# A recommender tower on one core: sums of a tile taken in PSUM, products on Pool, layer 0 spread out, six Y banks

## The chip, the cores and the metric

The kernel runs on one core of a Trainium2 chip. The metric is the device time of one execution in microseconds. Before the change it is 732.16 us, the median of three runs (731.63 to 733.88).

## The reference, cut to what matters

For each of 512 samples, 40 embedding rows of 16 numbers are gathered from 40 tables (`e`, 512 x 40 x 16). Three layers follow, then a small dense network:

```
x = e
for k in (k0, k1, k2):                      # k0: 128x40x40, k1 and k2: 128x128x40
    x = einsum('bhd,bmd,ohm->bod', x, e, k) # outer product with e, mixed by k
    outputs.append(x.sum(-1))
h = concat(outputs + [dense_ctx])           # 512 x (3*128 + 16)
h = relu(h @ W_top1 + b1); h = relu(h @ W_top2 + b2); y = h @ W_top3
```

All data is fp32.

## The kernel before, in words

A token is a pair (sample, d); there are 8192. They are worked in 16 groups of 512 tokens (32 samples), a group in four tiles of 128 tokens, so 64 tiles T.

Per group, the preparation: Pool gathers the rows (ten indirect DMAs per group, L220); SP stores them into a scratch in HBM (six DMAs, L188), and loads them back (L191, L196) as A3 (the 40 fields three times, 120 rows) and as seven rolled copies `pairs`. DVE multiplies each copy with A3 (L359), which gives all products of two fields. Layer 0 is seven matmuls into the bank X1: three of them split into a high and a low fp32r part (L280 on ACT, L366 on DVE, three passes each at L475 to L477), four in plain fp32 (L481, two passes each). X1 is then split into x1hi (ACT, L283) and x1lo (DVE, L370), and summed over d into z0 (DVE, L373). PE also transposes A3 into xtok (L462, L271), the token's 40 field values as per-partition scalars.

Per tile, layer 1: ten chunks c0 to c9 of 512 columns (four m by 128 outputs). Each is three fp32r matmuls into one of five PSUM banks Y (L515 to L517). Each quarter of a chunk is then multiplied by its xtok scalar and all 40 quarters are summed. ACT owns six chunks (OWNER "ADAADAADAD") and writes the scaled values to SBUF (`scaled`, L318). DVE owns four and accumulates as it multiplies (L427). Pool adds three of ACT's results (`fold`, L257), and DVE merges all into x2 (L392, four steps). Then G = x2 against a diagonal pattern `diag` (Pool, L247) gives, per sample, what layer 2 and the sums need: two half-height matmuls (L491), copied by ACT (L286).

The steps of the next group's preparation are dealt into the stream of chunks by a table of positions (`position`, `prep_steps`): p counts a group's 40 chunks on each engine. A hardware loop runs three bodies of four groups; the fourth body stands unrolled behind it. After the last group, layer 2 and the dense network follow (L531 to L557).

What orders the engines are counting semaphores: chunk c of a tile may not start before its bank's earlier chunk has been read; s_l0, s_x1free and s_xtok guard X1, TR and xtok; s_merge, s_diag and s_Gout guard G.

Of the kernel before, what the change touches and what calls it, by code (L numbers as in the profile page):

```python
# [30 lines left out]
NA, ND = OWNER.count("A"), OWNER.count("D")
STT = ND * MB
FOLDS = 3
EXTRA = NA - 2 - FOLDS
MERGE = EXTRA + 3
NS = 3
# [2 lines left out]
XTOK_AT, PROD_AT, PROD_APART, L0_LAG = 14, 6, 3.6, 6
SPLIT_LAG = {"ph": 1, "pl": 2}  # L40
X1_LAG = {"x1hi": 1, "x1lo": 2, "z0": 3}
GATHER_TILES = 3
MERGE_AT = (0, 3, 3, 3)
G_AT = 8
def position(step):
    if step == "xtok":
        return XTOK_AT
    if step in X1_LAG:
        return position(f"l0_{NC0 - 1}") + X1_LAG[step]
    kind, c = step[:-1], int(step[-1])  # L50
    if kind in ("l0_", "prod"):
        return int(PROD_AT + PROD_APART * c) + (L0_LAG if kind == "l0_" else 0)
    return int(PROD_AT + PROD_APART * c) + SPLIT_LAG[kind]
def prep_steps():
    names = ["xtok"]
    for kind, n in (("prod", NC0), ("ph", NS), ("pl", NS), ("l0_", NC0)):
        names += [f"{kind}{c}" for c in range(n)]
    names += X1_LAG
    return sorted(names, key=position)
def rank(c):  # L60
    return OWNER[:c + 1].count(OWNER[c])
def chunk(u, slot, c):
    k = NC0 * (slot + 1) + c
    return GPB * NC0 * u + k, k % NR, GPB * NC0 // NR * u + k // NR
def split(u, slot, c):
    k = NS * (slot + 1) + c
    number = NC0 * (GPB * u + slot + 1) + c
    free = number - NH + 1 if c >= NH else number - NC0 + NS - NH + 1 if slot >= 0 else None
    return GPB * NS * u + k, k % NH, free
def build(nc, ids, first_row, table, k0a, k0b, k1, k2, ctxT, w1, w1c, b1, w2, b2, w3, ident_in, mask_in,  # L70
# [7 lines left out]
    with ctx:  # L78
# [24 lines left out]
        scaled = sb("scaled", [P, NA, BANK])  # L103
        fold = [sb(f"fold{i}", [P, BANK]) for i in range(2)]
        chain = [sb(f"chain{i}", [P, BANK]) for i in range(2)]
# [1 line left out]
        diag = [sb(f"diag{i}", [P, MH, HB]) for i in range(2)]
        G = sb("G", [P, MH, SB + B])
# [496 lines left out]
```

## Time and profile before

| | us |
|---|---|
| median of the runs | 732.16 |
| the profiled execution | 735.69 |
| its span | 733.9 |
| PE busy | 672.8 (92%) |
| DVE busy | 609.3 (83%) |
| POOL busy | 526.9 (72%) |
| ACT busy | 520.1 (71%) |

One execution was profiled. Busy times of an engine are unions, so overlapping instructions count once. PE busy includes the modelled ends of pipelined matmuls. A stretch of the loop is best read from the first Y matmul of one group (L515) to that of the next.

### The profile page before, as it was taken

How to read it: one execution, taken by the hardware profiler on the slowest of the kernel's cores; microseconds unless marked ns; L12 is line 12 of the kernel's file. 1: busy time of each engine (PE TensorE's matmuls, PEld its weight loads, DVE VectorE, ACT ScalarE, POOL GpSimd, SP SyncE). 2: the span in 40 equal slices, each digit the busy share in tenths (PEclk: the TensorE clock that was granted, in tenths of full speed). 3: DMA queues.
4: the chain of work that ended last, by engine and by line, in shares of the span. 5: the costliest groups of instructions: out<-in, count | busy, mean ns of one | idle time of the engine just before them, and what ended most of it. 6: DMA issues, size and time to landing. Idle time of an engine off the chain costs nothing.

```text
span 733.9 us, 13319 instructions
## 1 busy us (share of the span) xinstructions
PE 672.8 (92%) x2752; PEld 472.9 (64%) x2752; DVE 609.3 (83%) x1542; ACT 520.1 (71%) x1753; POOL 526.9 (72%) x443
## 2 busy tenths in 40 slices
PE   0379999999989999999999999999999999998998
PEld 0246767677666766676667767676767676773583
DVE  1649898888989898989798998989898989888290
ACT  1338777777777777778777777687778787886293
POOL 6538888998979798988789888888797874552000
PEclk9999999999999999999999999999999999997799
DMA  6361120302031212122120303031312121100000
GB/s 203 98 232 50 37 83 13 108 10 97 20 89 29 79 40 76 44 59 60 26 95 10 96 19 100 17 90 29 84 36 78 43 77 41 47 1 29 0 1 0
DMA packets 56679, 43.08 MB, mean 59 GB/s; under 512 B 37007, under 2 KB 40335, under 8 KB 56352
## 3 DMA queue, kind: packets, MB, share of 16 engines
q1 hardware_dynamic: 51488, 41.08, 18.5%
q0 software_dynamic: 5120, 1.32, 1.9%
q14 instruction: 59, 0.48, 0.2%
q8 instruction: 12, 0.20, 0.1%
HBM read 40.41 MB, written 1.97 MB: 58 GB/s over the span
## 4 chain that ended last, share of the span: by engine, by line
issue 33%; POOL 29%; PE 27%; DVE 6%; DMA 3%; SPq 1%; POOLq 1%; ACT 1%; DVEq 0%; ACTq 0%
POOL x0g L220 17%; POOL fold L257 9%; PE Y L515 5%; PE Y L517 5%; PE Y L516 5%; DVE chain L427 2%; POOL diag L247 2%; PE X L481 2%; DMA pairs<-scratch 2%; DVE pairs L359 1%; PE X L542 1%; PE X L540 1%; PE X L541 1%; DVE chain L392 1%; PE GB L491 1%
## 5 line engine op out<-in xcount | busy, mean ns | idle before, releaser
L318 ACT ACTIVATE scaled<-Y,xtok 128x128 f32<-128x128 f32 x1536 | 421.1, 380 | 107.1 <-PE Y L517 106.3
L515 PE MATMUL Y<-k1lo,x1hi 128*128 128x512 f32 x640 | 290.4, 454 | 20.1 <-DVE chain L427 18.6
L517 PE MATMUL Y<-k1hi,x1lo 128*128 128x512 f32 x640 | 253.1, 396 | 0.0
L516 PE MATMUL Y<-k1hi,x1hi 128*128 128x512 f32 x640 | 252.5, 395 | 0.0
L220 POOL DMA_INDIRECT x0g<-in_table,rows_now x160 | 221.0, 1381 | 42.2 <-issue 37.8
L427 DVE SCALAR_TENSOR_TENSOR chain<-Y,xtok,chain 128x128 f32<-128x128 f32 x768 | 213.0, 339 | 23.7 <-PE Y L517 23.7
L257 POOL TENSOR_TENSOR fold<-fold,scaled 128x512 f32<-128x512 f32 x128 | 183.8, 1436 | 12.5 <-ACT scaled L318 0.6
L515 PEld LDWEIGHTS Y<-k1lo,x1hi 128*128 128x128 f32 x640 | 120.5, 188 | 80.4 <-DVE chain L427 37.0
L516 PEld LDWEIGHTS Y<-k1hi,x1hi 128*128 128x128 f32 x640 | 121.0, 189 | 35.6 <-issue 14.4
L517 PEld LDWEIGHTS Y<-k1hi,x1lo 128*128 128x128 f32 x640 | 120.6, 188 | 30.3
L359 DVE TENSOR_TENSOR pairs<-pairs,A 120x512 f32<-120x512 f32 x112 | 108.9, 973 | 30.9 <-DMA pairs<-scratch 30.9
L257 POOL TENSOR_TENSOR fold<-scaled 128x512 f32<-128x512 f32 x64 | 84.4, 1318 | 68.7 <-ACT scaled L318 68.7
L427 DVE SCALAR_TENSOR_TENSOR chain<-Y,xtok,scaled 128x128 f32<-128x128 f32 x256 | 71.8, 342 | 5.1 <-PE Y L517 4.0
L481 PE MATMUL X<-pairs,w 120*128 120x512 f32 x128 | 65.6, 594 | 1.7 <-DVE pairs L359 1.7
L280 ACT ACTIVATE pairs_hi<-pairs 120x512 fp32r<-120x512 f32 x48 | 30.3, 632 | 47.5 <-DVE pairs L359 47.5
L392 DVE TENSOR_TENSOR chain<-chain,scaled 128x512 f32<-128x512 f32 x65 | 44.9, 691 | 7.9 <-ACT scaled L318 4.8
L475 PE MATMUL X<-pairs_lo,w0hi 120*128 120x512 f32 x48 | 22.6, 470 | 30.2 <-DVE pairs_lo L366 30.2
L392 DVE TENSOR_TENSOR chain<-chain,fold 128x512 f32<-128x512 f32 x65 | 44.3, 681 | 0.0
L366 DVE TENSOR_TENSOR pairs_lo<-pairs,pairs_hi 120x512 fp32r<-120x512 f32 x48 | 40.5, 843 | 3.0 <-ACT pairs_hi L280 3.0
L491 PE MATMUL GB<-diag,x 64*128 64x164 f32 x260 | 36.1, 354 | 6.2 <-DVE x L392 6.2
L491 PEld LDWEIGHTS GB<-diag,x 64*128 64x128 f32 x260 | 19.8, 186 | 30.3 <-issue 22.3
L247 POOL TENSOR_TENSOR diag<-xtok,mask 128x160 f32<-128x160 f32 x64 | 35.5, 555 | 2.8 <-POOL rows_now L216 1.9
(77 smaller groups left out, 460.3 us busy)
## 6 DMA issues: line engine op xcount, KB each, us to landing
pairs<-scratch SPq DMA_DIRECT2D x112, 240.0 KB
A<-scratch SPq DMA_DIRECT2D x16, 240.0 KB
k1raw<-in_k SPq DMA_DIRECT2D x1, 2560.0 KB, 10.8
x0g<-in_table,rows_now POOLq DMA_INDIRECT x160, 2.8
k2s<-in_k SPq DMA_DIRECT2D x1, 2560.0 KB, 9.2
scratch<-x0g SPq DMA_DIRECT2D x96, 20.0 KB, 1.7
pairs<-in_w SPq DMA_DIRECT2D x3, 256.0 KB, 3.0
w2s<-in_w SPq DMA_DIRECT2D x1, 512.0 KB, 3.9
```

The costliest lines, as they stand in the source:

```text
L220: nc.gpsimd.indirect_dma_start(x0g[buf][:, f, :], None, table, bass.IndirectOffsetOnAxis(ap=rows_now[buf][:, f:f + 1], axis=0)).then_inc(s ...
L247: nc.gpsimd.tensor_tensor(diag[tile % 2][:, 0:M, :], xtok[slot % 2][:, j, :].unsqueeze(2).to_broadcast([P, M, HB]), mask[:, :].unsqueeze(1 ...
L257: nc.gpsimd.tensor_tensor(sums[:, :], scaled[:, 1, :] if a == 2 else sums[:, :], scaled[:, a, :], ALU.add).then_inc(s_fold, 1)
L318: ins = nc.scalar.activation(scaled[:, rank(c) - 1, i * O:(i + 1) * O], Y[(NCH * tile + c) % YB][:, i * O:(i + 1) * O], ACT.Copy, scale=xt ...
L359: nc.vector.tensor_tensor(pairs[buf][0:PR, :], pairs[buf][0:PR, :], A3[par][0:PR, :], ALU.mult).then_inc(s_prod, 1)
L392: nc.vector.tensor_tensor(to, a, b, ALU.add).then_inc(s_merge, 1)
L427: nc.vector.scalar_tensor_tensor(out=chain[tile % 2][:, i * O:(i + 1) * O], in0=Y[(NCH * tile + c) % YB][:, i * O:(i + 1) * O], scalar=xto ...
L481: nc.tensor.matmul(X1[:, :], w0[:, (c - NS) * O:(c - NS + 1) * O], pairs[buf][0:PR, :], start=False, stop=(c == NC0 - 1)).then_inc(s_l0, 1)
L491: ins = nc.tensor.matmul(GB2[:, h, 0:MH * HB], x2[buf][rows, :], diag[buf][rows, :, :].rearrange("p m b -> p (m b)"), start=True, stop=True)
L515: nc.tensor.matmul(y, hi[:, tok], k1lo[:, cols], start=True, stop=False)
L516: nc.tensor.matmul(y, hi[:, tok], k1hi[:, cols], start=False, stop=False)
L517: nc.tensor.matmul(y, lo[:, tok], k1hi[:, cols], start=False, stop=True).then_inc(s_y, 1)
```

## The change

The loop is gone: all 64 tiles are written out. There are six Y banks; G has one bank, and the transposes go through X1 (`TR = X1`). ACT owns seven chunks (OWNER "AADAAADAAD": 0, 1, 3, 4, 5, 7, 8), DVE three (2, 6, 9). ACT scales chunk 0 into SBUF (`first`) and the other six in place, in their PSUM banks. DVE starts with chunk 2 on top of `first`, adds ACT's chunks straight from PSUM, and ends with chunk 9, whose four quarters it writes back into the bank and reduces into x2. Pool no longer folds; it makes the products of the next group (of the first group, DVE does) and a `diag` of double width for one full-height G matmul. Layer 0 is seven plain fp32 matmuls at chunks 5, 9, 14, 18, 22, 27, 31 of the group before. `pairs` has seven buffers. At the start, ACT issues half of the first group's stores and loads, and PE runs 20 matmuls on k1hi whose results are not used. k2s is loaded after group 2's loads.

```diff
-YB = 5
-OWNER = "ADAADAADAD"
+YB = 6
+OWNER = "AADAAADAAD"
+WARM = 20
+XTOK_PE_AT, XTOK_AT = 1, 3
+L0_AT = (5, 9, 14, 18, 22, 27, 31)
+X1HI_AT = 33
+G_AT, GCOPY_AT = 4, 5
+PRODUCTS_OF_TILE = ((0, 1, 2), (3, 4, 5), (6,), ())
+GATHERS_OF_TILE = ((0, 3), (3, 6), (6, 10), (0, 0))
+STEPS = ("mac2", "mac2", "mac2", "mac2", "sum1", "sum3", "sum4", "mac6", "mac6", "mac6", "mac6", "sum5",
+         "sum7", "sum8", "mac9", "mac9", "mac9", "mac9", "quarters")
...
 @block.sync
+            for r in range(0, ROLLS // GF, 2):
+                store_copy(sp, 0, r)
+            sp.wait_ge(s_scratch, 16 * (ROLLS // GF))
+            sp.dma_start(A3[0][0:PR, :], rolled_rows(0, 0, 0)).then_inc(s_a3, 16)
+            for c in range(0, NC0, 2):
+                load_roll(sp, 0, c)
...
 @block.gpsimd
+            for g in range(NG):
+                for j in range(TPG):
+                    T = TPG * g + j
+                    pool.wait_ge(s_xtok, g + 1)
+                    if T >= 2:
+                        pool.wait_ge(s_G, T - 1)
+                    nc.gpsimd.tensor_tensor(diag[T % 2][:, 0:M, :], ...
+                    if j == 0 and g + 2 < NG:
+                        take_rows(g + 2, g % 2)
+                    if g + 1 < NG:
+                        for c in PRODUCTS_OF_TILE[j]:
+                            product(g + 1, c)
+                    if g + 2 < NG:
+                        gather(g % 2, range(*GATHERS_OF_TILE[j]))
...
 @block.scalar
+                        for i in range(MB):
+                            m, o = c * MB + i, slice(i * O, (i + 1) * O)
+                            ins = nc.scalar.activation(first[:, o] if c == 0 else y[:, o], y[:, o], ACT.Copy,
+                                                       scale=xtok[g % 2][:, j, m:m + 1])
...
 @block.vector
+            def add_scaled(T, c):
+                dve.wait_ge(s_yA, act_count(T, c))
+                nc.vector.tensor_tensor(chain[:, :], chain[:, :], Y[(NCH * T + c) % YB][:, :],
+                                        ALU.add).then_inc(s_chain, 1)
...
+                nc.vector.tensor_reduce(x2[T % 2][:, :], Y[(NCH * T + 9) % YB][:, :].rearrange(
+                    "p (m o) -> p o m", o=O), AX.X, ALU.add).then_inc(s_chain, 1)
...
 @block.tensor
+                    if k >= YB:
+                        wait_for_bank(k)
...
+                        if p == XTOK_PE_AT:
+                            pe.wait_ge(s_a3, 16 * (g + 2))
+                            pe.wait_ge(s_x1free, g + 1)
+                            transposes(g + 1)
+                        elif p in L0_AT:
+                            if p == L0_AT[0]:
+                                pe.wait_ge(s_xtok, g + 2)
+                            pe.wait_ge(s_prod, NC0 * g + L0_AT.index(p) + 1)
+                            layer0(L0_AT.index(p))
+                    if c == G_AT and T > 0:
+                        make_G(T - 1)
```

How the instructions stand on DVE at the end of a group, first before (the group's last tile up to the next group's first multiply-adds; chain1 and chain0 are the sums of the two tiles, Y the banks, fold1 Pool's sum):

```order
L427 SCALAR_TENSOR_TENSOR chain1<-Y4,xtok1,chain1 128x128 [waits chain_steps,y_filled]
L427 SCALAR_TENSOR_TENSOR chain1<-Y4,xtok1,chain1 128x128 [waits chain_steps] x3
L370 TENSOR_TENSOR x1lo0<-X1,x1hi0 128x512 [waits x1_high_ready]
L373 TENSOR_REDUCE z0<-X1 128x32
L427 SCALAR_TENSOR_TENSOR chain1<-Y2,xtok1,chain1 128x128 [waits chain_steps,y_filled]
L427 SCALAR_TENSOR_TENSOR chain1<-Y2,xtok1,chain1 128x128 [waits chain_steps] x3
L427 SCALAR_TENSOR_TENSOR chain1<-Y4,xtok1,chain1 128x128 [waits chain_steps,y_filled]
L427 SCALAR_TENSOR_TENSOR chain1<-Y4,xtok1,chain1 128x128 [waits chain_steps] x3
L392 TENSOR_TENSOR chain1<-chain1,scaled 128x512 [waits y_emptied_by_act,chain_steps]
```

Now the same place, from chunk 6 of the group's last tile on (chain is the one sum, Y3 at the end the bank of chunk 9):

```order
L338 TENSOR_TENSOR chain<-chain,Y4 128x512 [waits y_scaled_by_act,chain_steps]
L332 SCALAR_TENSOR_TENSOR chain<-Y0,xtok1,chain 128x128 [waits y_filled,chain_steps]
L332 SCALAR_TENSOR_TENSOR chain<-Y0,xtok1,chain 128x128 x3
L302 TENSOR_TENSOR x1lo0<-X1,x1hi0 128x512 [waits x1_high_ready]
L338 TENSOR_TENSOR chain<-chain,Y5 128x512 [waits y_scaled_by_act,chain_steps]
L338 TENSOR_TENSOR chain<-chain,Y1 128x512 [waits y_scaled_by_act,chain_steps]
L305 TENSOR_REDUCE z0<-X1 128x32
L338 TENSOR_TENSOR chain<-chain,Y2 128x512 [waits y_scaled_by_act,chain_steps]
L332 SCALAR_TENSOR_TENSOR Y3<-Y3,xtok1,chain 128x128 [waits y_filled,chain_steps]
L332 SCALAR_TENSOR_TENSOR Y3<-Y3,xtok1,chain 128x128 x3
L370 TENSOR_REDUCE x2_1<-Y3 128x128 [waits g_filled,chain_steps]
```

Before, only the tile's own multiply-adds on chunk 4 stand ahead of x1lo, with z0 right behind it. Now the adds of ACT's chunks 1, 3 and 4 (the last of them is the first row) and the multiply-adds on chunk 6 stand ahead of x1lo, and two more adds ahead of z0.

On ACT, x1hi in the group's last tile, before:

```order
L318 ACTIVATE scaled<-Y2,xtok1 128x128 [waits y_filled,pool_folds]
L318 ACTIVATE scaled<-Y2,xtok1 128x128 x3
L318 ACTIVATE scaled<-Y3,xtok1 128x128 [waits y_filled,pool_folds]
L318 ACTIVATE scaled<-Y3,xtok1 128x128 x3
L283 ACTIVATE x1hi0<-X1 128x512 [waits l0_done]
L318 ACTIVATE scaled<-Y0,xtok1 128x128 [waits y_filled,pool_folds]
L318 ACTIVATE scaled<-Y0,xtok1 128x128 x3
```

and now:

```order
L265 ACTIVATE first<-Y0,xtok0 128x128 [waits y_filled,chain_steps]
L265 ACTIVATE first<-Y0,xtok0 128x128 x3
L265 ACTIVATE Y1<-Y1,xtok0 128x128 [waits y_filled]
L265 ACTIVATE Y1<-Y1,xtok0 128x128 x3
L265 ACTIVATE Y3<-Y3,xtok0 128x128 [waits y_filled]
L265 ACTIVATE Y3<-Y3,xtok0 128x128 x3
L229 ACTIVATE x1hi1<-X1 128x512 [waits l0_done]
L265 ACTIVATE Y4<-Y4,xtok0 128x128 [waits y_filled]
L265 ACTIVATE Y4<-Y4,xtok0 128x128 x3
```

x1hi is behind chunk 3 both times; the chunks beside it now go back to their own banks and wait for no fold.

## Rows read from the trace of the kernel before

**Rows 1.** Busy times by stretch: five groups, the work behind the last G

```profile
43.67:84.47 40.80, 39.35 (x161) 28.41 (x162) 33.82 (x89) 29.50 (x105) 31.51 (x24) 0.96 0.26 73
162.89:202.09 39.20, 37.88 (x163) 27.24 (x161) 35.28 (x92) 29.80 (x106) 33.77 (x27) 1.00 0.20 57
202.09:242.89 40.80, 37.90 (x162) 27.32 (x161) 36.45 (x92) 29.86 (x106) 33.88 (x27) 1.00 0.20 55
556.97:595.09 38.12, 37.75 (x162) 27.16 (x161) 35.03 (x92) 29.79 (x107) 31.11 (x28) 1.00 0.21 59
634.02:668.36 34.34, 30.89 (x137) 23.23 (x135) 28.89 (x89) 30.25 (x107) 17.89 (x17) 0.99 0.07 24
668.36:733.90 65.54, 62.63 (x176) 33.85 (x176) 33.43 (x50) 33.24 (x54) 0.00 (x0) 0.85 0.03 8
```

Columns: stretch, its length, busy us (and instructions) of PE, PEld, DVE, ACT, POOL, granted clock, share of the DMA engines, GB/s.

**Rows 2.** The same view, the first and the fourth tile of one group

```profile
162.89:170.57 7.68, 7.68 (x36) 5.86 (x34) 5.27 (x17) 5.71 (x21) 5.35 (x6) 1.00 0.41 118
192.69:202.09 9.40, 9.40 (x40) 6.62 (x38) 8.04 (x23) 7.38 (x27) 8.44 (x7) 1.00 0.07 9
```

**Rows 3.** Timeline, PE, one chunk and the next one's start (start, us, instruction)

```profile
162.89 0.40 PE L515 MATMUL Y<-k1lo,x1hi 128*128 128x512 f32 x1
...
163.36 0.39 PE L517 MATMUL Y<-k1hi,x1lo 128*128 128x512 f32 x1
163.59 0.40 PE L515 MATMUL Y<-k1lo,x1hi 128*128 128x512 f32 x1
```

**Rows 4.** Timeline, the end of the last tile and the last G

```profile
664.94 1.13 DVE L427 SCALAR_TENSOR_TENSOR chain<-Y,xtok,chain 128x128 f32<-128x128 f32 x4 [0.96 <-PE Y L517]
...
666.11 0.69 DVE L392 TENSOR_TENSOR chain<-chain,scaled 128x512 f32<-128x512 f32 x1
666.83 0.69 DVE L392 TENSOR_TENSOR chain<-chain,fold 128x512 f32<-128x512 f32 x1
...
668.36 0.92 PE L491 MATMUL GB<-diag,x 64*128 64x164 f32 x4 [3.46 <-DVE x L392]
```

**Rows 5.** Groups of instructions by line and shape (busy us, mean ns | idle before)

```profile
L318 ACT ACTIVATE scaled<-Y,xtok 128x128 f32<-128x128 f32 x1536 | 421.1, 380 | 107.1 <-PE Y L517 106.3 <-DVE chain L427 0.7
...
L283 ACT ACTIVATE x1hi<-X 128x512 fp32r<-128x512 f32 x16 | 10.3, 644 | 8.2 <-PE X L481 8.2
...
L373 DVE TENSOR_REDUCE z<-X 128x512 f32 x12 | 8.2, 681 | 0.0
```

**Rows 6.** Timeline, the start: first stores, A load, first and seventh product

```profile
17.63 2.86 SPq L188 DMA_DIRECT2D scratch<-x0g  x6
22.28 0.91 SPq L191 DMA_DIRECT2D A<-scratch  x1
...
27.72 0.69 DVE L359 TENSOR_TENSOR pairs<-pairs,A 120x512 f32<-120x512 f32 x1 [3.40 <-DMA pairs<-scratch]
...
40.30 0.69 DVE L359 TENSOR_TENSOR pairs<-pairs,A 120x512 f32<-120x512 f32 x1 [1.76 <-DMA pairs<-scratch]
```

**Rows 7.** Busy times by stretch, while the first loads run

```profile
24.00:28.00 4.00, 0.00 (x0) 0.00 (x0) 0.60 (x2) 0.00 (x0) 2.84 (x4) 1.00 0.71 203
```

**Rows 8.** Timeline, POOL and DVE, two gathers and what DVE does beside them

```profile
302.64 2.15 DVE L427 SCALAR_TENSOR_TENSOR chain<-Y,xtok,chain 128x128 f32<-128x128 f32 x8
...
304.00 0.98 POOL L220 DMA_INDIRECT x0g<-in_table,rows_now  x1
...
305.29 1.51 POOL L220 DMA_INDIRECT x0g<-in_table,rows_now  x1 [0.30 <-issue]
305.31 0.68 DVE L392 TENSOR_TENSOR chain<-chain,scaled 128x512 f32<-128x512 f32 x1
```

**Rows 9.** Pool's lines by themselves (ns min/median/max)

```profile
L220 POOL DMA_INDIRECT x0g<-in_table,rows_now x160: 940/1327/2542, 3.4 to 590.4; - x160
...
DMA to landing us min/median/max: 2.2/2.8/7.3
...
L257 POOL TENSOR_TENSOR fold<-fold,scaled x128: 1266/1296/1690, 51.1 to 664.6; 128x512 f32<-128x512 f32 x128
```

More of the change, by code:

```diff
@@ L28, with chain_count, act_count @@
 NCH = M // MB
-YB = 5
-OWNER = "ADAADAADAD"
[L31 to L36, printed above, removed]
+YB = 6
+OWNER = "AADAAADAAD"
+NA = OWNER.count("A")
 CTX = 16
 H1, H2 = 512, 256
[L39 to L69, printed above, removed]
+WARM = 20
[7 more added lines that the diff above has]
+         "sum7", "sum8", "mac9", "mac9", "mac9", "mac9", "quarters")
+NSTEP = len(STEPS)
+def chain_count(T, name):
+    return NSTEP * (T + 1) - STEPS[::-1].index(name)
+def act_count(T, c):
+    return NA * T + OWNER[:c + 1].count("A")
 def build(nc, ids, first_row, table, k0a, k0b, k1, k2, ctxT, w1, w1c, b1, w2, b2, w3, ident_in, mask_in,
@@ L102, in build @@
         xtok = [sb(f"xtok{i}", [P, TPG, M]) for i in range(2)]
[L103 to L105 removed]
+        first = sb("first", [P, BANK])
+        chain = sb("chain", [P, BANK])
         x2 = [sb(f"x2_{i}", [P, O]) for i in range(2)]
[L107 to L108 removed]
+        diag = [sb(f"diag{i}", [P, MH, SB]) for i in range(2)]
+        G = sb("G", [P, MH, B])
         z0 = sb("z0", [P, B])
@@ L226, in _ @@
                 gather(g, range(GF))
-            for i in range(2):
-                nc.gpsimd.memset(diag[i][:, :, :], 0.0).then_inc(s_dzero, 1)
-            pool.wait_ge(s_dzero, 2)
             pool.wait_ge(s_const, 32)
@@ L327, in _, with k1_high @@
-            over_groups(act, body)
+                    G[:, :, T * SB:(T + 1) * SB],
+                    GB[:, 0:MH * SB].rearrange("p (m b) -> p m b", b=SB), ACT.Copy).then_inc(s_Gout, 1)
+            def k1_high(c):
+                nc.scalar.activation(k1hi[:, c * BANK:(c + 1) * BANK], k1raw[:, c, :], ACT.Copy).then_inc(s_k1hi, 1)
+            act.wait_ge(s_k1, 16)
+            k1_high(0)
+            act.wait_ge(s_gather[0], 16 * GF)
+            for r in range(1, ROLLS // GF, 2):
+                store_copy(act, 0, r)
@@ new lines, in _, with mac @@
+            x1_low(0)
+            z0_sums(0)
+            def mac(T, c):
+                y, x = Y[(NCH * T + c) % YB], xtok[T // TPG % 2]
+                to = y if c == NCH - 1 else chain
+                dve.wait_ge(s_y, NCH * T + c + 1)
+                for i in range(MB):
+                    m, o = c * MB + i, slice(i * O, (i + 1) * O)
+                    nc.vector.scalar_tensor_tensor(
+                        out=to[:, o], in0=y[:, o], scalar=x[:, T % TPG, m:m + 1],
+                        in1=first[:, o] if c == 2 else chain[:, o],
+                        op0=ALU.mult, op1=ALU.add).then_inc(s_chain, 1)
@@ L441, in _ @@
+            dve.wait_ge(s_chain, chain_count(NTILES - 1, "quarters"))
             for c in range(NCH):
@@ L483, in make_G @@
-            def make_G(T, buf, xtok=None):
-                pe.wait_ge(s_merge, MERGE * (T + 3))
-                pe.wait_ge(s_diag, T + 2)
-                pe.wait_ge(s_Gout, T + 2)
-                if xtok is not None:
-                    pe.wait_ge(s_xtok, xtok)
-                for h in range(2):
-                    rows = slice(h * (P // 2), (h + 1) * (P // 2))
-                    ins = nc.tensor.matmul(GB2[:, h, 0:MH * HB], x2[buf][rows, :], diag[buf][rows, :, :].rearrange(
-                        "p m b -> p (m b)"), start=True, stop=True)
-                ins.then_inc(s_G, 1)
@@ L523, in _, with transposes, layer0 @@
-            over_groups(pe, body)
-            make_G(NTILES - 1, (NTILES - 1) % 2)
+            def transposes(g):
+                for j in range(TPG):
+                    ins = nc.tensor.transpose(TR[:, j * PR:(j + 1) * PR], A3[g % 2][0:PR, j * P:(j + 1) * P],
+                                              ident[0:PR, 0:PR])
+                ins.then_inc(s_trans, 1)
+            def layer0(c):
+                nc.tensor.matmul(X1[:, :], w0[:, c * O:(c + 1) * O], pairs[c][0:PR, :],
+                                 start=(c == 0), stop=(c == NC0 - 1)).then_inc(s_l0, 1)
```

485 lines of the change are left out of this document (189 added, 296 removed).

## The prediction, made before the changed kernel ran

> **What bounds the kernel now.** I read the busy times by stretch first, cutting the span at the first Y matmul of each group. A middle group takes 39.20 us and PE is busy for 37.88 of them; every fourth group, after the loop branches back, takes 40.80; a group of the body that stands behind the loop takes 38.12 [rows 1]. DVE shows 35 us in the same stretches, ACT under 30. So PE is the bound, with little waiting. By tile it is plainer: a tile with nothing beside its ten chunks and its G takes 7.68 us, and one with two unsplit layer-0 matmuls 9.40, so one of those costs (9.40 - 7.68) / 2 = 0.86 [rows 2]. A chunk is 0.70, and its result is there (163.36 - 162.89) + 0.39 = 0.86 after it starts [rows 3]. Ten chunks are 7.0, which leaves 0.68 for G.
>
> PE's work of one group before: 4 x 7.68 = 30.72, four unsplit matmuls 3.44, three split ones about 0.8 each (three passes of 0.23 [rows 3] and the change of kind), transposes about 0.8 (an estimate): 37.4. Of the 39.20, 1.8 is waiting. That is all that the loop can give back on PE's side; 15 groups run from 43.67 to 634.02, 590.35 us. The last group, without preparation, takes 34.34 to the last G, of which 3.46 is PE waiting for the merges [rows 1, 4]. Behind it come 65.54 [rows 1]. Span 733.9; the execution took 735.69, 3.53 above the median shown, and the sum is made against it.
>
> **The loop: PE.** 30.72 stays: G has two passes of 328 columns in place of four of 164, the same columns (0.55 if only columns count, 0.80 if the taller operand costs; I keep 0.68). Layer 0 is now seven unsplit matmuls, 7 x 0.86 = 6.02 in place of 5.87. Transposes give 120 columns instead of 40: four at 120/512 of 0.86 are 0.8 (0.8 to 1.6; I take 0.9). Sum 37.64 per group. The change removes next to no PE work; it moves the waits.
>
> **The loop: DVE.** A block of four multiply-adds and the dependent operation behind it are 666.11 - 664.94 = 1.17 apart, two dependent adds 666.83 - 666.11 = 0.72 [rows 4]; 512 columns read from PSUM take 681 ns [rows 5]. A tile is three blocks, six adds and the quarter sum: 3 x 1.17 + 6 x 0.72 + 0.68 = 8.51. With x1lo and z0 a group has 4 x 8.51 + 1.4 = 35.4, under PE's 37.64. Two forms are not in the trace: multiply-adds that write PSUM (0.26 apart to 0.34 unoverlapped, +0.3 a tile at most), and a reduce over a stride of 128 columns (0.68 to twice that). I take the low ends, which are the rows of the same size; at the high ends a group has 39.3, and both covers are gone.
>
> **The loop: ACT.** 28 activations a tile in place of 24, 24 of them back into PSUM, for which there is no row. Those into SBUF cost 421.1 / 1536 = 0.274 each in a stream and 0.380 alone [rows 5]. Bounds: 0.09 (what 128 more columns add between 380 and 644 ns for 128 and 512) to 0.38. At 0.274 a group is 112 x 0.274 = 30.7 plus six copies of at most 0.65 = 34.6: covered.
> The Trainium skill, "PSUM — Partial Sum Buffer", Specifications, says ScalarE writes PSUM faster than SBUF. No row here shows it; by it this term could only shrink.
>
> **Where PE will wait.** X1 is one bank for layer 0, transposes, x1hi, x1lo and z0, so two waits stand at each group's start. In the fourth tile the last layer-0 matmul pushes c3 to 0.70 + 0.70 + 0.86 + 0.70 = 2.96. Its result is there at 3.86. On ACT: c3's four activations 4 x 0.27 = 1.08, the x1hi copy 0.53 (0.64 less the overlap of 0.11), c4's four 3 x 0.27 + 0.38 = 1.19: 6.7. On DVE: sum4 0.72, mac6 1.08, x1lo 0.70: 9.2. The tile's PE work ends at 7.68 + 0.86 = 8.54: PE waits 0.7 for x1lo. Then two chunks, and the transposes want z0 at 10.6; sum5 0.72, sum7 0.69 and z0 0.72 bring it at 11.3: 0.7 more. Banks cost nothing elsewhere: with six of them, c0 waits for sum4, c1 for sum5 and c5 for the quarters of the tile before, all at least 0.5 ahead by the same sums. A group is 37.64 + 1.4 = 39.0.
> Fifteen groups: 15 x 37.64 + 15 x 0.7 + 14 x 0.7 = 584.9, and 0.6 for a part of the low clock (granted 0.96 in the first group before [rows 1]; I expect the warm-up matmuls to take off more than half of 1.6 us): 585.5, -4.9.
>
> **The last group.** No layer 0 stretches PE here, so DVE sets the end. From the group's first chunk (x1lo just done) sum5, sum7, z0, sum8, mac9 and the quarters of the old tile take 4.7, then four tiles 34.0: the last G starts at 38.7 in place of 34.34, +4.4. The 65.54 behind it keep their instructions; PE waits before G, as it did.
>
> **The start.** Before, six stores go out by one queue in 2.86, the A load at 22.28, the first product comes at 27.72 and the seventh at 40.30, since each waits for the split of the one before and for four buffers [rows 6]. Now two queues send three stores each: A at 20.9. Seven buffers, no split; DVE puts a k1lo piece (0.7) between products, so they are 1.39 apart: from 26.8 to 35.1, end 35.8. The 2.68 from the last product's end to the first chunk stay: 38.5 in place of 43.67. I take -5.0. If the layer-0 matmuls run at half clock here (1.72 each), they lag the products by 6 x 0.33 + 0.86: -2.1.
> The loads are not what the second queue helps: DMA engines are 71% busy at 203 GB/s while only SP has loads out [rows 7], and eight loads of 240 KB at that rate take 9.7 us, 22.6 (1.7 behind A, as 22.28 to 24.0 before) to 32.3, ahead of the last product.
> The Trainium skill, "DMA: Bandwidth & Descriptors", Issuing engines are not separate DMA queues, says a second issuing engine saves issue time alone; the row agrees. A reader who gave the second queue twice the rate would end the loads near 27.5, and still be held by DVE's 1.39.
>
> **Pool and the loads.** Products go to Pool, folds leave it. From one group's first product to the next one's: seven products at 1.30, two diag at 0.81 (320/512 of it), ten gathers at 0.95 + 0.30, 1.55 until the last lands (2.8 less 1.25), 4.65 from the stores to A, 5.44 from A to a product [rows 6, 8, 9]: 34.8, under 39.0, and the first layer-0 matmul comes only after six chunks. Cost nothing. This counts on undisturbed Pool rows: a gather beside multiply-adds takes 0.98, one beside an add of two SBUF tiles 1.51 [rows 8], and DVE's new loop has no operation with two SBUF tiles.
>
> **Sum.** 735.69 - 5.0 - 4.9 + 4.4 = 730.2; less 3.5, 726.5 for the median. Own range 718 to 732.
>
> **The rivals.**
> 1. ACT finishes its PSUM chunks sooner. If each activation is 0.1 shorter, c3 and c4 end 0.8 sooner, x1lo waits for nothing and z0 for little: 15 x 0.8 less, 714. For: this chain is what holds DVE in the fourth tile. Against: the duration is unmeasured here.
> The Trainium skill's rule on PSUM writes ("PSUM — Partial Sum Buffer", Specifications) points this way.
> 2. No change: waits stay at the 1.8 per group that they are now, 39.4 each, +6: 732. For: DVE is as full as before, 35 us. Against: the unrolled group of 38.12 shows that the loop itself held PE.
> 3. Slower by Pool: products and gathers disturb each other or DVE. With products at 1.69 and gathers at 1.33 + 0.30 [rows 9] the ring is 41.5 and sets the pace: +2.5 x 14 = 35, 762. It decides from 39.0. For: the new ring carries products, gathers, stores and loads in series. Against: the slow rows lie beside DVE adds that are gone.
> 4. Slower by ACT: activations that read and write one bank don't overlap. Beyond (39.0 - 3.9) / 112 = 0.313 each, ACT sets the pace; at 0.34 a group is 42.0, 772. For: no row has this form. Against: those into SBUF overlap freely.
> 5. The change doesn't do what it says: warm-up doesn't hold the clock through the start. Then -2.1 and no 1.0 in the first group, 730.5; in the forecast's range.
>
> **How the numbers follow.** Forecast 0.49, rival 1 0.14, rival 2 0.16, rival 3 0.13, rival 4 0.08 (rival 5 within the first). About 0.3% (2.2 us) is what a measurement of this kernel can tell from no change. Faster: rival 1, most of the forecast (0.43) and some of rival 2 (0.03): 0.60. Same: 0.06 and 0.11: 0.17. Slower: rivals 3 and 4 and 0.02: 0.23. The range goes from 712, under rival 1, to 745, which takes in rival 2 and a mild form of rival 3; rival 4 and the full rival 3, a little under 0.2, are left out.
>
> **What would show it.** First Y matmul near 38.5; groups of 39.0 with two gaps before PE, one after x1lo and one after z0 (the transposes), each about 0.7, none elsewhere; DVE tiles of 8.5; PE idle several us in each tile of the last group and the last G 38.7 after that group's start; gathers of 0.95 throughout and no wait of a layer-0 matmul for a product. Wrong if a group is under 38 (waits gone) or over 40 with PE waiting for banks, products or ACT.

## The result, and the profile after

The changed kernel takes 708.18 us (median of 4 runs, 706.59 to 709.77) where the kernel before took 733.02 beside it: ratio 0.9657, 95% interval 0.962 to 0.9694. Forecast were 726.5 and a range from 712: the sign was right, the size was not. The profiled execution took 707.73 (span 705.9); the prediction's sum for it was 730.2.

Busy times by stretch, after (the columns of [rows 1]): the first group, two middle ones, the last, the work behind the last G.

```profile
38.57:75.43 36.86, 36.21 (x145) 26.57 (x145) 29.84 (x71) 30.58 (x115) 21.94 (x23) 1.00 0.27 83
188.27:225.87 37.60, 36.66 (x146) 26.88 (x146) 33.45 (x79) 31.75 (x120) 21.45 (x23) 1.00 0.23 66
225.87:263.49 37.62, 36.68 (x147) 26.88 (x147) 33.45 (x79) 31.81 (x120) 21.46 (x23) 1.00 0.20 56
602.08:640.17 38.09, 31.96 (x129) 23.45 (x129) 36.70 (x86) 34.57 (x125) 2.22 (x3) 1.00 0.12 37
640.17:705.90 65.73, 62.87 (x174) 33.98 (x174) 33.45 (x50) 33.24 (x54) 0.00 (x0) 0.84 0.00 0
```

Against [rows 1]: the first Y matmul is 5.1 earlier, the last group 3.75 longer, the tail the same. The rest is the fifteen groups between, 602.08 - 38.57 = 563.51 in place of 590.35: 26.8 less, where 4.9 were forecast. All but the first are alike to 0.02; DVE is busy about 2 us less in each, Pool 12.

The waits of PE in the same trace (us in total, times, longest):

```profile
PE Y L435 <- DVE x1lo L302: 10.4, 16, 1.4
PE GB L401 <- DVE x L370: 5.7, 5, 4.2
PE X L388 <- DVE z L305: 4.9, 14, 0.4
```

Inside the groups only the two waits are left that the prediction named. With the weight loads that they hold up they are 0.88 and 0.53 a group, 1.41 (worked out from the starts of the matmuls around them). So PE's work is 37.6 - 1.4 = 36.2, not 37.64.

Some executions keep the clock full behind the last G and are about 10 us shorter than others of the same kernel; the table below therefore gives the fifteen groups of the profiled execution too, which that does not touch (b_Gtall's median and b_allPE's ratio lean on such executions; the ratio of b_allPE's medians is 0.984).

### The profile page after: what moved, and what is told of

Read it like the earlier page. It is cut to its first block, busy times and chain, and to the rows that moved or that the text cites. A ratio compares the mean times of both kernels' runs of the same rounds, so it can differ in the third digit from the quotient of the medians.

```text
span 705.9 us, 10117 instructions
## 1 busy us (share of the span) xinstructions
PE 658.9 (93%) x2528; PEld 467.6 (66%) x2528; DVE 581.7 (82%) x1316; ACT 550.7 (78%) x1957; POOL 336.5 (48%) x351
## 4 chain that ended last, share of the span: by engine, by line
PE 74%; DVE 12%; ACT 8%; issue 2%; DMA 2%; POOL 1%; SPq 0%; ACTq 0%; DVEq 0%
PE Y L437 16%; PE Y L435 16%; PE Y L436 16%; PE X L392 13%; ACT Y L265 6%; DVE chain L338 5%; PE GB L401 4%; DVE chain L332 3%; DVE z L305 1%; PE X L466 1%; PE X L464 1%; PE X L465 1%; PE X L388 1%; POOL x0g L184 1%; ACT x1hi L229 1%
## 5 line engine op out<-in xcount | busy, mean ns | idle before, releaser
L265 ACT ACTIVATE Y<-Y,xtok 128x128 f32<-128x128 f32 x1536 | 420.6, 382 | 56.0 <-PE Y L437 56.0
L338 DVE TENSOR_TENSOR chain<-chain,Y 128x512 f32<-128x512 f32 x384 | 263.6, 686 | 49.9 <-ACT Y L265 40.9
L437 PE MATMUL Y<-k1hi,x1lo 128*128 128x512 f32 x640 | 251.8, 393 | 0.0
L436 PE MATMUL Y<-k1hi,x1hi 128*128 128x512 f32 x640 | 250.7, 392 | 0.0
L184 POOL DMA_INDIRECT x0g<-in_table,rows_now x160 | 153.9, 962 | 42.1 <-issue 37.2
L205 POOL TENSOR_TENSOR diag<-xtok,mask 128x320 f32<-128x320 f32 x64 | 47.3, 740 | 230.0 <-PE GB L401 214.5
L436 PEld LDWEIGHTS Y<-k1hi,x1hi 128*128 128x128 f32 x640 | 120.7, 189 | 46.1 <-issue 21.6
L197 POOL TENSOR_TENSOR pairs<-pairs,A 120x512 f32<-120x512 f32 x105 | 133.0, 1290 | 13.6 <-DMA pairs<-scratch 12.6
L437 PEld LDWEIGHTS Y<-k1hi,x1lo 128*128 128x128 f32 x640 | 120.2, 188 | 26.2
L392 PE MATMUL X<-pairs,w 120*128 120x512 f32 x224 | 115.4, 596 | 2.2 <-DVE pairs L320 1.8
L265 ACT ACTIVATE first<-Y,xtok 128x128 f32<-128x128 f32 x256 | 73.1, 368 | 35.9 <-DVE chain L338 25.3
L332 DVE SCALAR_TENSOR_TENSOR chain<-Y,xtok,chain 128x128 f32<-128x128 f32 x256 | 72.1, 345 | 9.8 <-PE Y L437 7.9
L332 DVE SCALAR_TENSOR_TENSOR Y<-Y,xtok,chain 128x128 f32<-128x128 f32 x256 | 72.6, 353 | 2.3
L332 DVE SCALAR_TENSOR_TENSOR chain<-Y,xtok,first 128x128 f32<-128x128 f32 x256 | 71.6, 343 | 2.4 <-PE Y L437 2.4
```

The costliest lines, as they stand in the source:

```text
L184: nc.gpsimd.indirect_dma_start(x0g[buf][:, f, :], None, table, bass.IndirectOffsetOnAxis(ap=rows_now[buf][:, f:f + 1], axis=0)).then_inc(s ...
L197: nc.gpsimd.tensor_tensor(pairs[c][0:PR, :], pairs[c][0:PR, :], A3[g % 2][0:PR, :], ALU.mult).then_inc(s_prod, 1)
L205: nc.gpsimd.tensor_tensor(diag[T % 2][:, 0:M, :], xtok[g % 2][:, j, :].unsqueeze(2).to_broadcast([P, M, SB]), mask[:, :].unsqueeze(1).to_b ...
L265: ins = nc.scalar.activation(first[:, o] if c == 0 else y[:, o], y[:, o], ACT.Copy, scale=xtok[g % 2][:, j, m:m + 1])
L332: nc.vector.scalar_tensor_tensor(out=to[:, o], in0=y[:, o], scalar=x[:, T % TPG, m:m + 1], in1=first[:, o] if c == 2 else chain[:, o], op0 ...
L338: nc.vector.tensor_tensor(chain[:, :], chain[:, :], Y[(NCH * T + c) % YB][:, :], ALU.add).then_inc(s_chain, 1)
```

## The experiments

| run | median us | ratio to before (95%) | fifteen groups, us |
|---|---|---|---|
| before / after | 733.0 / 708.2 | 0.962 to 0.969 | 590.4 / 563.5 |
| b_noloop | 724.9 | 0.984 to 0.989 | 580.6 |
| b_fullG | 753.1 | 1.023 to 1.029 | 609.7 |
| b_fullG_tr | 753.5 | 1.023 to 1.029 | 609.1 |
| b_Gtall | 717.7 | 0.967 to 0.979 | 576.0 |
| b_tr | 723.3 | 0.980 to 0.990 | 575.4 |
| b_pad32 | 724.7 | 0.983 to 0.991 | 580.5 |
| b_allPE | 721.6 | 0.965 to 0.977 | 574.7 |
| a_G4 | 709.2 | 0.955 to 0.966 | 563.9 |
| a_tr40 | 716.0 | 0.971 to 0.978 | 572.0 |
| a_pad32 | 714.0 | 0.969 to 0.976 | 569.5 |
| a_5banks | 722.6 | 0.976 to 0.986 | 577.3 |
| a_x1early | 701.3 | 0.952 to 0.957 | 555.7 |
| a_x1early_G | 701.8 | 0.950 to 0.957 | 556.8 |
| a_sbuf | 763.7 | 1.033 to 1.043 | 619.6 |
| a_best | 691.7 | 0.938 to 0.946 | 556.4 |

Names with b_ start from the kernel before, with a_ from the changed one. The fifteen groups are those of one execution each. The edits are shown in short form. My theory after the result: PE's work in a group is smaller than I had priced, and the loop itself held PE. The rival: DVE and Pool, with their new division of the sums, set the new pace.

**The loop (b_noloop).**

```diff
-            with eng.Fori(0, BODIES - 1) as u:
+            for u in range(BODIES - 1):
                 body(u, False)
```

> The kernel before with its sixteen groups written out, no hardware loop; nothing else changes. Theory (the loop itself held PE): the three intervals of 40.6 to 40.8 behind a branch back come to 39.2, 4.7 us in all, and the twelve looped groups come to the mean of the ones written out (39.47, 38.12, 38.93: 38.8), 12 x 0.4 = 4.8: 9.5 us off, about 723.5. Rival 1 (the branch alone costs): 4.7 off, 728. Rival 2 (the last groups are quicker only for being last, and PE's waits move elsewhere): 0 to 2 off, 731 to 733.

9.85 us less than before beside it: the theory's number. Two groups of it by busy times:

```profile
199.43:237.54 38.11, 37.74 (x162) 27.15 (x161) 35.39 (x92) 29.78 (x107) 31.07 (x28) 1.00 0.22 58
237.54:277.02 39.48, 37.88 (x163) 27.20 (x161) 35.31 (x92) 29.81 (x107) 32.44 (x28) 1.00 0.21 56
```

A looped group took 39.2, and 40.8 behind a branch [rows 1]; now most take 38.1, some 39.5. That is 9.8 of the 26.8.

**G, transposes and the pitch of a chunk, measured.** First PE's timeline in b_noloop, which has before's forms, around the transposes and around a G (start, us, instruction):

```profile
211.18 0.39 PE L517 MATMUL Y<-k1hi,x1lo 128*128 128x512 f32 x1
211.41 0.99 PE L462 MATMUL GB<-ident,A 120*128 120x40 f32 x8
212.22 0.47 PE L515 MATMUL Y<-k1lo,x1hi 128*128 128x512 f32 x1
212.54 0.40 PE L516 MATMUL Y<-k1hi,x1hi 128*128 128x512 f32 x1
...
293.26 0.40 PE L517 MATMUL Y<-k1hi,x1lo 128*128 128x512 f32 x1
293.59 0.55 PE L491 MATMUL GB<-diag,x 64*128 64x164 f32 x4
294.07 0.50 PE L515 MATMUL Y<-k1lo,x1hi 128*128 128x512 f32 x1
294.40 0.40 PE L516 MATMUL Y<-k1hi,x1hi 128*128 128x512 f32 x1
```

A record is one row of the profile's instructions; x8 stands for eight. Then the changed kernel's G, and its transposes in a_x1early, where no wait stands in front of them:

```profile
192.55 0.40 PE L437 MATMUL Y<-k1hi,x1lo 128*128 128x512 f32 x1
192.79 0.71 PE L401 MATMUL GB<-diag,x 128*128 128x328 f32 x2
193.09 0.64 PE L435 MATMUL Y<-k1lo,x1hi 128*128 128x512 f32 x1
193.57 0.39 PE L436 MATMUL Y<-k1hi,x1hi 128*128 128x512 f32 x1
```

```profile
224.85 0.40 PE L437 MATMUL Y<-k1hi,x1lo 128*128 128x512 f32 x1
225.08 0.57 PE L388 MATMUL X<-ident,A 120*128 120x120 f32 x4
225.42 0.48 PE L435 MATMUL Y<-k1lo,x1hi 128*128 128x512 f32 x1
225.74 0.39 PE L436 MATMUL Y<-k1hi,x1hi 128*128 128x512 f32 x1
```

From the last matmul ahead (L517, L437) to the second one behind (L516, L436) it is 0.469 before and 0.458 after where nothing stands between (medians). G makes that 1.143 and 1.012, so it costs 0.674 before, 0.554 after; the transposes make it 1.357 and 0.887: 0.888 and 0.429. The pitch of a chunk, from its start to that of the next with nothing between, is 0.700 and 0.687:

```profile
236.81 0.39 PE L435 MATMUL Y<-k1lo,x1hi 128*128 128x512 f32 x1
...
238.87 0.39 PE L435 MATMUL Y<-k1lo,x1hi 128*128 128x512 f32 x1
```

That is three chunks of the changed kernel, 2.06; the same three in a_pad32 (below) take 2.11:

```profile
239.26 0.40 PE L436 MATMUL Y<-k1lo,x1hi 128*128 128x512 f32 x1
...
241.37 0.40 PE L436 MATMUL Y<-k1lo,x1hi 128*128 128x512 f32 x1
```

**Put back into the changed kernel (a_G4, a_tr40, a_pad32).**

```diff
-    nc.tensor.matmul(GB[:, 0:MH * SB], x2, flat_diag, ...)
+    for h in range(2):    # a_G4: flat = diag as p (m b), half = 164
+        nc.tensor.matmul(GB[:, cols_of(h)], x2, flat[:, cols_of(h)], ...)
```

> The changed kernel with G as two column halves of 164 in place of one matmul of 328 columns; nothing else changes. Theory (G's cost falls with the number of passes: from the last chunk ahead of G to the second pass behind it, less the same without G, 0.674 before with four passes and 0.554 after with two): 0.12 a tile comes back on PE, except in the fourth tile of a group, where it shortens the wait for x1lo, and in the last group, where DVE sets the end: 15 x 3 x 0.12 = 5.4 more, about 713.5. Rival (the columns alone count, and the height of the operand made before's G dearer): no change, 708.

A miss: 1.0 us more, G 0.565. Cutting the same columns into twice the records does not matter; the rival stands, and points to the height.

```diff
-    nc.tensor.transpose(TR[:, j * PR:(j + 1) * PR], A3[...], ident[0:PR, 0:PR])
+    nc.tensor.matmul(TR[:, j * M:(j + 1) * M], A3[...], ident[0:PR, 0:PR:KC], start=True, stop=True)  # a_tr40
```

> The changed kernel with the four transposes of a group as matmuls of 40 columns against a strided identity, as the kernel before has them. Theory (they cost 0.89 a group as eight records and 0.43 as four of 0.103): 0.46 a group more on PE's path, 15 x 0.46 = 6.9, about 715. Rival 1 (the prediction's prices, 0.8 and 0.9): 1 to 2 us less. Rival 2 (hidden, since the wait for z0 stands in front of them and DVE sets the group): no change.

7.8 more, 38.15 a group: as expected.

```diff
+        pad = sb("pad", [P, 8])   # a_pad32 and b_pad32
         k1hi = sb("k1hi", [P, M * O], f32r)
```

> The changed kernel with an unused tile of 32 bytes a partition ahead of k1hi, so that k1hi and k1lo (and the small tiles behind them) begin 32 bytes past a multiple of 64, as in the kernel before. Theory (where the streamed operand begins sets the pitch of a chunk): the pitch between PE's first and second pass goes from 0.226 to 0.231 back to 0.237, a chunk from 0.687 to 0.700, 15 x 40 x 0.012 = 7 more, about 715. Rival (something else of the new program does it): the pitches stay, 708.

5.8 more. The median from PE's first to its second pass goes from 0.231 to 0.238, the next one from 0.229 to 0.231: to the nanosecond what they were before. A group is 37.95, not 38.1, since a later chunk shortens the wait for x1lo.

**Taken out of the kernel before (b_fullG, b_fullG_tr, b_Gtall, b_tr, b_pad32, b_allPE).** All are without the loop. b_fullG doubles diag and mask and makes one G matmul:

```diff
-    for h in range(2): matmul(GB2[:, h, 0:MH * HB], x2[buf][rows, :], diag[buf][rows, ...])
+    matmul(GB[:, 0:MH * SB], x2[buf][:, :], diag[buf][...])
```

> As the run without the loop, and G as one matmul of full height and 328 columns in place of two of half height and 164; diag and mask twice as wide. Theory (G costs by columns and passes, 0.54 in place of 0.68 per tile, and PE is the bound): 64 x 0.14 = 9 us less than the run without the loop, about 714.5. Rival 1 (my prediction's term, G keeps its 0.68): 0, the same as the run without the loop. Rival 2 (the freed time turns into a wait for DVE, which already held PE 55.6 us of the span): 0 to 3 us less, and the idle time before the chunks grows by what G loses.

> As the run with the full-height G, and the four transposes of a group as transposes of 120 columns in place of matmuls of 40 columns against a strided identity. Theory (one pass of 0.103 each, where the matmuls took about 0.2 each): 15 x 0.35 to 0.45 = 5 to 7 us less, about 708.5. Rival 1 (the prediction's 0.9 a group in place of 0.8: three times the columns): 1 to 2 us more than the run before it. Rival 2 (absorbed by waits for DVE): 0.

Both wrong, and by the most: 28 slower. DVE's last quarter sum by line and shape, in b_noloop and in b_fullG:

```profile
L392 DVE TENSOR_TENSOR x<-chain 128x128 f32<-128x128 f32 x65 | 24.6, 379 | 2.2
```

```profile
L392 DVE TENSOR_TENSOR x<-chain 128x128 f32<-128x128 f32 x65 | 88.3, 1358 | 2.2
```

It has its operands in SBUF and now meets Pool's longer diag (0.79 in the mean, 0.48 in b_noloop) and the folds behind it: 0.98 more a tile, and DVE sets a pace of 40.7. So the full G was not to be had with these sums as they stood.
The Trainium skill's "SBUF — State Buffer", Terms, calls the read and write ports that DVE and GpSimd share exclusive for a whole instruction; 1358 in place of 379 agrees.
 
To see the height by itself, b_Gtall leaves diag as it is:

```diff
-    GB2[:, h, 0:MH * HB], x2[buf][rows, :], diag[buf][rows, :, :]
+    GB2[:, h, 0:MH * HB], x2[buf][:, :], diag[buf][:, :, :]
```

> The kernel before without its loop, and each of G's two matmuls taken over all 128 rows of its operands in place of 64 (so every column of G sums both halves of a tile, which the reference does not); columns, diag and all other engines as they were. Theory (the half-height operands made before's G dear: 0.674 a tile with them, while two full-height column halves cost 1.023 - 0.458 = 0.565 in the changed kernel): 0.11 less a tile on PE, which is the bound, 60 x 0.11 = 6.6 less than the run without the loop, about 718. Rival 1 (the half-height pairs run side by side, so the tall ones cost twice the streaming): 4 x 164 columns in place of 2 x 164, 0.14 more a tile, about 733. Rival 2 (absorbed by waits for DVE): 725.

G falls to 0.55 (1.018 less 0.463 to 0.469): the half-height operands were dear, the theory's size. The groups give 4.6 of the expected 6.6. In three tiles of a group the gain arrives; in the other, from the starts of the matmuls, the layer-0 matmul behind the next chunk comes 0.13 later, which takes it up.

b_tr has the four transposes of the changed kernel (the diff of a_tr40 the other way), b_pad32 the pad.

> The kernel before without its loop, and the four transposes of a group as transposes of 120 columns in place of matmuls of 40 columns against a strided identity; G as before. Theory (0.43 a group in place of 0.89, on PE's path): 15 x 0.46 = 6.9 less than the run without the loop, about 718. Rival (the waits for DVE take it up): 724 to 725.

> The kernel before without its loop, and the same 32 bytes ahead of k1hi, so that k1hi and k1lo begin on a multiple of 64. Theory (as above, the other way): a chunk goes from 0.700 to 0.687; PE's floor is 0.5 a group lower, of which the waits for DVE take up a part as they did with the cheaper transposes: 3 to 7 less than the run without the loop, 718 to 722. Rival: the pitches stay, 725.

In the profiled executions the groups shrink by 5.2 with the transposes and by 0.1 with the pad. The 5.2 is in part chance: b_tr's profiled execution was its shortest and b_noloop's its longest, and their medians differ by 1.6. The commonest group is 38.1 in both; from the starts of the matmuls, the transposes take 0.48 less and the wait in front of the next layer-0 matmul 0.48 more. So this is the rival.

The pad did not do what the theory said. The first to second pass falls to 0.233, but eight chunks with nothing between them take 5.57:

```profile
199.58 0.40 PE L516 MATMUL Y<-k1lo,x1hi 128*128 128x512 f32 x1
...
205.15 0.39 PE L516 MATMUL Y<-k1lo,x1hi 128*128 128x512 f32 x1
```

That is 0.697 each, beside 0.700 in b_noloop and 0.687 in the changed kernel. So it is not enough that k1hi and k1lo begin on a multiple of 64 bytes. Counted from the sizes of the tiles ahead, they begin on a multiple of 128 in the changed kernel, 64 past one in b_pad32, 32 past one in the kernel before and in a_pad32; no run tells whether that is the reason. All three cuts at once:

> The kernel before without its loop, with all three cuts of PE's work at once: the 32 bytes ahead of k1hi, transposes of 120 columns, and G's two matmuls over all 128 rows (every column of G then sums both halves of a tile, which the reference does not). The sums of a tile stay as they were, with folds on Pool and products on DVE. Theory (PE's lighter work alone makes the gain, 0.5 + 0.46 + 4 x 0.125 = 1.46 a group): 15 x 1.46 = 22 less than the run without the loop, about 703. Rival (DVE, 35.3 busy a group and disturbed by Pool's folds, holds a group near 37.8 however little PE has to do): 715 to 719, with PE's idle time before the chunks grown to over 1 a group.

5.9 of the 22 in the groups: the rival. But 7.5 of the 22 was the pad's, and a chunk stays near 0.697 here too. Of the 14 that the other two cuts were worth, more than half is lost in waits: most groups stand at 37.85, and PE waits (in all, times, longest), first in b_noloop, then here:

```profile
PE X L475 <- DVE pairs_lo L366: 28.9, 2, 28.7
```

```profile
PE X L475 <- DVE pairs_lo L367: 34.9, 17, 29.5
PE Y L514 <- DVE chain L428: 10.1, 20, 1.4
```

The longest of pairs_lo is the start; the rest is new. With the old sums, splits and folds, much of what PE saves becomes waiting for DVE. PE's lighter work is needed, as a_tr40 and a_pad32 show, and so is DVE's.

**What keeps DVE and Pool apart (a_sbuf).**

```diff
-    act(first if c == 0 else y, y, scale=...)      dve: chain + Y
+    act(first if c == 0 else scaled[a], y, scale=...)  dve: chain + scaled[a]
```

> The changed kernel with ACT's six scaled chunks a tile written to SBUF tiles in place of their PSUM banks; DVE adds them from there, so its six adds a tile have two operands in SBUF. Theory (the sums straight from PSUM are what keeps DVE and Pool apart; rival 3 of the prediction applies to adds of two SBUF tiles): gathers go from 0.96 to 1.2 or more, products from 1.29 to 1.4 or more, DVE's adds from 0.69 to about 0.85, DVE's group from 35.4 to 35.4 + 24 x 0.16 = 39.3, so that DVE sets the pace: 39.5 to 40 a group, +30 to 35, about 740. Rival 1 (only Pool suffers, and its ring of 34.8 has room): DVE's adds stay at 0.69, no change, 708. A look besides: if ACT's and DVE's traffic in SBUF is what made a chunk 0.700 before in place of 0.687, the pitch between PE's first and second pass goes from 0.231 to 0.238 here.

55 slower, more than the theory's 30 to 35. Groups of instructions in it:

```profile
L340 DVE TENSOR_TENSOR chain<-chain,scaled 128x512 f32<-128x512 f32 x384 | 358.8, 934 | 16.9 <-ACT scaled L267 4.0
...
L198 POOL TENSOR_TENSOR pairs<-pairs,A 120x512 f32<-120x512 f32 x105 | 171.1, 1653 | 11.4 <-DMA pairs<-scratch 10.4
L185 POOL DMA_INDIRECT x0g<-in_table,rows_now x160 | 169.9, 1062 | 42.2 <-issue 38.6 <-POOL rows_now L181 0.6
```

and the same in the changed kernel:

```profile
L338 DVE TENSOR_TENSOR chain<-chain,Y 128x512 f32<-128x512 f32 x384 | 263.6, 686 | 49.9 <-ACT Y L265 40.9
...
L184 POOL DMA_INDIRECT x0g<-in_table,rows_now x160 | 153.9, 962 | 42.1 <-issue 37.2 <-POOL rows_now L180 0.6 <-DMA pairs<-scratch 0.3
L197 POOL TENSOR_TENSOR pairs<-pairs,A 120x512 f32<-120x512 f32 x105 | 133.0, 1290 | 13.6 <-DMA pairs<-scratch 12.6
```

One operand from PSUM in place of SBUF, and DVE's add is 0.25 shorter, Pool's product 0.36. A group of a_sbuf takes 41.1, and DVE is busy for 39.9 of them: its 24 adds are 24 x 0.25 = 6.0 longer, on the 35.4 of the prediction's count. A chunk stays at 0.687, so ACT's target has no part in that.

**The banks and the waits (a_5banks, a_x1early, a_x1early_G).**

```diff
-YB = 6
+YB = 5   # a_5banks; the last layers use another bank
```

> The changed kernel with five Y banks in place of six (the sixth serves only the last layers). Theory (the sixth bank is what keeps DVE's lag off PE: with five, the fifth chunk of a tile waits for the quarter sum of the tile before, which in the changed kernel ends 0.51 after that chunk's start in the first tile of a group, 0.05 after it in the second, ahead of it in the others): 0.6 to 0.8 a group, 15 x 0.7 = 10.5 more, about 718.5. Rival (DVE makes up the lag later in the group, since its work of 35.4 is under the 37.6): no change to 3 us, 708 to 711. A look besides: whether the pitch of a chunk (0.687 after, 0.700 before) follows the number of banks.

14.4 more, 0.9 a group: about the theory's size, mostly at another place. PE's waits:

```profile
PE Y L436 <- DVE chain L339: 19.4, 15, 1.3
PE Y L436 <- DVE x L371: 5.8, 18, 0.7
```

The second is the fifth chunk's for the quarter sum, 0.28 in a group. The first is at the group's start: with five banks c0 waits for sum5, which stands behind x1lo on DVE, 1.29 where x1lo alone held it 0.65. The wait for z0 is covered by these.

```diff
-X1HI_AT = 33
+X1HI_AT = 32   # and in DVE's order: x1lo ahead of sum4's wait and mac6, z0 ahead of sum7
```

> The changed kernel with the users of the bank X1 moved ahead: ACT copies x1hi one chunk earlier (behind p=32 of the group), DVE takes x1lo ahead of sum4 and mac6, and z0 ahead of sum7. Theory (what is left above PE's 36.24 a group is the two waits for x1lo and z0, 1.39 a group, as the prediction worked them out): the waits fall to about 0.25, 15 x 1.1 = 17 us off, about 692. Rival 1 (DVE, at 35.4 of work a group, takes over the pace at once, with waits for sum4 and sum5 at c0 and c1 in place of those removed): under 5 us off, 704 to 708. Rival 2 (x1hi ahead of ACT's scaling delays DVE's chain by as much as it gains): no change, 708.

6.9 less: the middle. Both waits go (0.2 stays at a group's start), but G of the tile before now waits 0.6 for its quarter sum; a group is 37.12.

```diff
-    if c == G_AT and T > 0:   # on top of a_x1early
+    if c == G_AT + (j == 0) and T > 0:   # and GCOPY_AT likewise
```

> The run with the users of X1 moved ahead, and G of the tile before a group one chunk later (behind the sixth chunk of the group, its copy too). Theory (what is left in that run above PE's 36.2 a group is the wait of this G for the quarter sum, 0.50 + 0.10, and 0.2 at the group's start): the first goes, 37.12 becomes 36.5, 15 x 0.6 = 9 less than that run, about 692. Rival 1 (DVE, with 35.4 of work and its own waits for ACT, can't go under 37 a group): no change, 701, and PE waits for a bank at c0 or c1 instead. Rival 2 (a part: the sixth bank's chunk waits): 695 to 698.

No change, 37.12 again (rival 1). The wait has moved to the bank of the quarters (first row), and DVE waits for ACT's scaled chunks (second, of DVE's own waits):

```profile
PE Y L435 <- DVE x L370: 5.7, 15, 0.8
```

```profile
DVE chain L338 <- ACT Y L265: 33.7, 91, 0.5
```

I read this as DVE's chain, 35.4 of work a group by the prediction's count and some 2 of waiting for ACT, setting the pace; no run takes ACT's part by itself.

**A version that beats both (a_best).** a_x1early, and

```diff
+            for i in range(16):
+                nc.tensor.matmul(X1[:, :], hi[:, 0:P], hi[:, :], start=True, stop=True)
             make_G(NTILES - 1)
```

> The run with the users of X1 moved ahead, and 16 matmuls of 512 columns into the free bank X1 (their sums are not used) ahead of the last G, where PE waits 4.15 for DVE in the changed kernel. Theory (that idle stretch is what halves the clock: granted 0.50 to 0.65 from 640.2 to 660 in the changed kernel, 21 us for work that takes half of that at full clock): the fillers take 16 x 0.231 = 3.7 of the 4.15, the clock stays at 1.00, about 10 less than the run without them, 691. Rival 1 (the clock falls all the same, since the fillers come after a first gap in each tile of the last group): 701. Rival 2 (the fillers end after the quarter sum is there, and push the last G back): 701 to 702 less what the clock gives.

691.67 us, 9.6 under a_x1early: the theory. The granted clock over the span, after and here:

```profile
PEclk9999999999999999999999999999999999996799
```

```profile
PEclk9999999999999999999999999999999999999999
```

In the changed kernel PE was idle for 4.15 ahead of the last G (3.46 in [rows 4]):

```profile
640.17 0.82 PE L401 MATMUL GB<-diag,x 128*128 128x328 f32 x2 [4.15 <-DVE x L370]
```

It then ran at 1.2 GHz (granted 0.50) from 644 to 660. Four of these us (the columns of [rows 1], PE alone), then the fillers of a_best:

```profile
644.00:648.00 4.00, 4.00 (x5) 0.50 0.00 0
```

```profile
629.25 3.80 PE L452 MATMUL X<-x1hi 128*128 128x512 f32 x16
```

Filled, the clock stays at 2.4 GHz (granted 1.00).

## Why the prediction was wrong in size

**The step that failed is "The loop: PE", its sum 37.64.** Measured it is 36.2, 1.45 less, and 15 x 1.45 = 21.8 is nearly all of the 730.2 - 707.7 = 22.5 that the sum missed. "The change removes next to no PE work" is what was wrong: by the same measured prices PE's work before was about 37.3 a group (40 chunks at 0.700, four G at 0.674, the transposes at 0.888, four layer-0 matmuls at 0.866 and three split ones at about 0.76), so the change takes 1.1 off it. That is 17 of the 26.8, as much as lies between b_noloop and the changed kernel (580.6 - 563.5), and the loop's 9.8 is the rest. The terms of the 37.64:
- G: "I keep 0.68" for the same columns. Measured 0.554, the low bound I had given (0.55). b_Gtall shows why: not the columns but the half-height operands made it 0.67 before. 4 x 0.13 = 0.5.
- Transposes: 0.9, bounds 0.8 to 1.6, from layer 0's price by columns. Measured 0.43, outside the bounds; four records of 0.103 for 120 columns, against eight of 0.112 for 40 before. The price followed the records, not the columns; the kind of instruction and the stride of the identity changed with them, and no run takes these apart. 0.47.
- The chunk: 0.70 taken as fixed. It fell to 0.687, 40 x 0.013 = 0.5. a_pad32 brings it back by 32 bytes of padding ahead of k1hi, so in the changed kernel it hangs on where k1hi, k1lo and the small tiles behind them lie; b_pad32 shows that a multiple of 64 bytes alone does not give it, and what does stays open. No row of before could show that.
- Layer 0: 7 x 0.866 = 6.06 for 6.02: right.

**Where PE waits** was right: 0.88 and 0.53 for 0.7 and 0.7, at the two places named, none elsewhere. So was the sixth bank (a_5banks). The prediction called a group under 38 a sign that these waits are gone; the group is 37.62 with both of them there, since it was the work that had been put too high. (c3's result in that working comes at 2.96 + 0.86 = 3.82, not 3.86; and 730.2 less 3.53 is 726.7, not 726.5. Neither changes the outcome.)

**The loop's own cost** I saw only as the "against" of rival 2. As the sum was built from work and waits it needed no such term, but [rows 1] had the sign of it: one unrolled group took 38.12 where the old groups took 590.35 / 15 = 39.36 in the mean. b_noloop gives 9.8 us for the loop alone.

**The start**: 38.57 for 38.5; first product at 26.82 for 26.8, seventh done at 35.97 where it began at 40.30 before [rows 6]. The 26.8 does not follow from its rows (20.9 + 5.44 = 26.3): A went out at 20.49 and the product came 6.33 behind it, so that hit is partly luck. The first group ran at granted 1.00 where it was 0.96 before, so rival 5 is out. **The last group**: 38.09 for 38.7, DVE setting the end. **The tail**: 65.73 for 65.54.

**ACT and DVE.** The forms without a row of before, by line:

```profile
L265 ACT ACTIVATE Y<-Y,xtok 128x128 f32<-128x128 f32 x1536 | 420.6, 382 | 56.0 <-PE Y L437 56.0
L265 ACT ACTIVATE first<-Y,xtok 128x128 f32<-128x128 f32 x256 | 73.1, 368 | 35.9 <-DVE chain L338 25.3 <-PE Y L437 10.6
L332 DVE SCALAR_TENSOR_TENSOR Y<-Y,xtok,chain 128x128 f32<-128x128 f32 x256 | 72.6, 353 | 2.3
L370 DVE TENSOR_REDUCE x<-Y 128x128 f32<-128x512 f32 x64 | 44.3, 692 | 2.2
```

In place into PSUM an activation takes 382 against 380 [rows 5] into SBUF, and overlaps as freely (420.6 / 1536 = 0.274): rival 4 is out, and so is rival 1, whose 714 came nearest for a reason that isn't there.
The Trainium skill's "PSUM — Partial Sum Buffer", Specifications, would have had it faster into PSUM; 382 beside 368 for the chunk into SBUF shows none of that.
The multiply-adds into PSUM (353) and the strided reduce (692) are at the low ends that I took.

**Pool.** Cost nothing, as said, and for the reason given: a_sbuf restores DVE operations with two SBUF operands, and the disturbance of rival 3 comes. Its mechanism does not: with products of 1.65, gathers of 1.06 + 0.30 and a diag of 0.90 Pool's ring is 11.6 + 13.6 + 1.8 + 11.6 = 38.6, under the 41.1, and PE waits for DVE and for no product of Pool. DVE's longer adds set the pace; that 41.1 is near the 41.5 that I had worked out for the ring is chance.

What stays open: why the half-height operands cost 0.12 more, what in the place of k1hi and k1lo sets the pitch of a chunk, and which chain of DVE, ACT and Pool holds the old sums at 37.85 in b_allPE.
